# Conditional expert-weight transfers in two mixture layers of a transformer on Trainium2

## What is computed

```
# first mixture: 8 experts, top 2, each token
h = silu(x @ Wg[e].T) * (x @ Wu[e].T)         # 192 -> 768, gated
out += (h @ Wd[e].T) * w_e                    # 768 -> 192
# second mixture: 16 experts, top 2, each token
h = gelu(x @ W1[e] + b1[e])                   # 192 -> 768
y += gate_e * (h @ W2[e] + b2[e])             # 768 -> 192
```

## Time and profile before

| what | value |
|---|---|
| median of 3 runs | 3248.65 us (3239.68 to 3267.87) |
| the profiled execution | 3244.56 us |
| its span in the trace | 3242.8 us |
| mean granted TensorE clock | 0.891 |
| TensorE busy | 2612.1 us (81%) |
| VectorE, ScalarE, GpSimd busy | 43%, 28%, 13% |
| moved by DMA | 235.89 MB, of it 199.45 MB on SyncE's queue |

### The profile page before, as it was taken

The page is one execution under the profiler, slowest core; times in us unless marked ns, Lnnn a source line. Parts: engine busy times, 40 slices in busy tenths (PEclk is TensorE's granted clock), DMA queues, the critical chain, the costliest instruction groups (busy, mean ns, idle before and its releaser), DMA issues. The chain is left out here.

```text
span 3242.8 us, 52613 instructions
## 1 busy us (share of the span) xinstructions
PE 2612.1 (81%) x17466; PEld 2210.3 (68%) x17466; DVE 1405.1 (43%) x3726; ACT 913.5 (28%) x2033; POOL 405.9 (13%) x502
## 2 busy tenths in 40 slices
PE   5876999974776688883999367999678989889895
PEld 5774888873665388882888256777357777777775
DVE  2346222226776611114222743555565363553634
ACT  1220111112553133331222012444123242342421
POOL 0001223220000133330000100000011010110200
PEclk8987999996997799996999657999679989999998
DMA  3012665641001298992000000000011303113021
GB/s 87 0 27 66 183 180 178 179 134 46 0 0 40 79 281 269 284 279 72 0 0 0 2 1 14 1 0 1 10 33 32 85 0 87 29 29 87 0 80 36
DMA packets 229468, 235.89 MB, mean 73 GB/s; under 512 B 33257, under 2 KB 206111, under 8 KB 229407
## 3 DMA queue, kind: packets, MB, share of 16 engines
q1 hardware_dynamic: 208638, 199.45, 21.5%
q0 software_dynamic: 12288, 29.38, 3.0%
q10 hardware_dynamic: 8480, 6.29, 0.8%
HBM read 213.81 MB, written 21.23 MB: 72 GB/s over the span
## 5 line engine op out<-in xcount | busy, mean ns | idle before, releaser
L870 PE MATMUL f_pg<-f_vxT,f_w 128*128 128x256 f32 (+1 forms) x1536 | 274.8, 333 | 17.2 <-DMA f_b<-in_L_ffn_b 8.4
L883 PE MATMUL f_po<-f_wd,f_hid 128*128 128x192 f32 x1536 | 270.5, 330 | 12.0 <-DMA f_b<-in_L_ffn_b 7.2
L870 PEld LDWEIGHTS f_pg<-f_vxT,f_w 128*128 128x128 f32 x1536 | 240.1, 193 | 46.0 <-issue 20.1
L883 PEld LDWEIGHTS f_po<-f_wd,f_hid 128*128 128x128 f32 x1536 | 249.0, 191 | 16.8 <-ACT f_hid L921 7.7
L840 POOL DMA_INDIRECT f_answers<-f_vout,f_to_row x128 | 126.9, 991 | 461.9 <-DVE f_vout L956 247.9
L2220 PE MATMUL s_bank<-s_disp,s_w 96*128 96x256 f32 x768 | 173.1, 382 | 7.1 <-DVE s_disp L2316 7.1
L921 ACT ACTIVATE f_hid<-f_pg,f_b 128x128 f32<-128x128 f32 x384 | 112.0, 369 | 236.8 <-PE f_pg L876 121.9
L2231 PE MATMUL s_bank<-s_hid,s_w 128*96 128x256 f32 x768 | 171.0, 379 | 0.0
L2220 PEld LDWEIGHTS s_bank<-s_disp,s_w 96*128 96x128 f32 x768 | 146.6, 191 | 29.9 <-DVE s_disp L2316 8.8
L944 DVE TENSOR_TENSOR f_hid<-f_silu,f_pg 128x256 f32<-128x256 f32 x192 | 72.3, 418 | 209.1 <-ACT f_silu L917 202.9
L917 ACT ACTIVATE f_silu<-f_pg 128x256 f32<-128x256 f32 x192 | 66.9, 383 | 336.4 <-issue 249.5
(11 more groups left out here) (369 smaller groups left out, 4896.4 us busy)
## 6 DMA issues: line engine op xcount, KB each, us to landing
f_wd<-in_L_ffn_W SPq DMA_DIRECT2D x64, 576.0 KB
s_w<-in_w SPq DMA_DIRECT2D x128, 288.0 KB, 3.4
f_w<-in_L_ffn_W SPq DMA_DIRECT2D x64, 384.0 KB
f_wd<-in_L_ffn_WdT SPq DMA_DIRECT2D x32, 576.0 KB
f_w<-in_L_ffn_WgT SPq DMA_DIRECT2D x32, 384.0 KB
f_w<-in_L_ffn_WuT SPq DMA_DIRECT2D x32, 384.0 KB
f_wr<-in_L_ffn_W SPq DMA_DIRECT2D x128, 96.0 KB
f_wr<-in_L_ffn_WgT SPq DMA_DIRECT2D x64, 96.0 KB
```

The lines of the kernel that those rows point to most:

```text
L870: pe.matmul(pg[j][:, a * ROWS:(a + 1) * ROWS], lift[a][r][:, j * 128:j * 128 + 128], xT[r][:, 0, :], start=(a == 0), stop=False, skip_grou ...
L883: last = pe.matmul(po[:, c * D:c * D + D], hid[r][:, j, c * 128:c * 128 + 128], wd[r][:, j, :], start=(at == 0), stop=(at == FC - 1))
```

## The change

`route` writes a second table, `fresh`: 1 for tile n if its expert differs from that of tile n-2 (the last user of the same buffers), 0 if not, and 1 for the first two tiles.

```diff
@@ route
             nc.vector.tensor_copy(expert_of[:], tile_expert[:])
+            nc.vector.tensor_tensor(passed[:, 2:NT], tile_expert[:, 2:NT], tile_expert[:, 0:NT - 2], ALU.not_equal)
+            link(nc.vector.memset(passed[:, 0:2], 1.0))
+            nc.vector.tensor_copy(fresh[:], passed[:])
@@ experts
-            def bring_lift(n, r, e):
+            def bring_lift(n, r, e, new):
                 sp.wait_ge(lifted, (n + 1) * PER)
                 for a, src in enumerate((w_in1, w_in2) if gated else (w_in1,)):
-                    sp.dma_start(lift[a][r][:], src[ds(e, 1), 0:128]...).then_inc(loaded[r], 16)
+                    sp.dma_start(lift[a][r][:], src[ds(e, 1), 0:128]..., cond=new).then_inc(loaded[r], 16)
...
-            def bring_down(n, r, e):
+            def bring_down(n, r, e, new):
...
-            def expert(n):
-                return sp.value_load(expert_of[0:1, ds(n, 1)], min_val=0, max_val=E - 1)
-
-            bring_lift(0, 0, expert(0))
+            def of_tile(n):
+                return (sp.value_load(expert_of[0:1, ds(n, 1)], min_val=0, max_val=E - 1),
+                        sp.value_load(fresh[0:1, ds(n, 1)], min_val=0, max_val=1))
+
+            bring_lift(0, 0, *of_tile(0))
             with sp.Fori(0, NT // 2 - 1) as i:
-                e = [expert(i * 2 + r) for r in range(3)]
-                bring_lift(i * 2 + 1, 1, e[1])
-                bring_down(i * 2, 0, e[0])
+                e = [of_tile(i * 2 + r) for r in range(3)]
+                bring_lift(i * 2 + 1, 1, *e[1])
+                bring_down(i * 2, 0, *e[0])
...
```

More of the change, by code:

```diff
@@ L420, in _, with route @@
                     nc.scalar.activation(xT[u][:], split2(pT[u][0:H2, 0:2 * D]), ACT.Copy).then_inc(copied, 1)
-def route(k, name, logits, wts, place_of, expert_of, E, ROWS, probs_first):
+def route(k, name, logits, wts, place_of, expert_of, fresh, E, ROWS, probs_first):
     nc = k.nc
@@ L737, in _, with experts @@
                                            op0=ALU.add, op1=ALU.add)
-def experts(k, name, normed, answers, from_row, to_row, expert_of, E, ROWS, w_in1, w_in2, w_down, b1, b2):
+def experts(k, name, normed, answers, from_row, to_row, expert_of, fresh, E, ROWS, w_in1, w_in2, w_down, b1, b2):
     nc = k.nc
@@ L788, in _ @@
         def _(sp):
-            def bring_lift(n, r, e):
+            def bring_lift(n, r, e, new):
                 sp.wait_ge(lifted, (n + 1) * PER)
                 for a, src in enumerate((w_in1, w_in2) if gated else (w_in1,)):
-                    sp.dma_start(lift[a][r][:], src[ds(e, 1), 0:128].rearrange("o p n -> p (o n)")).then_inc(loaded[r], 16)
+                    sp.dma_start(lift[a][r][:], src[ds(e, 1), 0:128].rearrange("o p n -> p (o n)"), cond=new).then_inc(loaded[r], 16)
                     for s in range(2):
@@ L822, in _ @@
-            bring_lift(NT - 1, 1, expert(NT - 1))
-            bring_down(NT - 2, 0, expert(NT - 2))
-            bring_down(NT - 1, 1, expert(NT - 1))
+                    sp.dma_start(down_bias[r][:], b2[ds(e, 1)].broadcast_to([128, D]), cond=new).then_inc(down_loaded[r], 16)
+            def of_tile(n):
+                return (sp.value_load(expert_of[0:1, ds(n, 1)], min_val=0, max_val=E - 1),
+                        sp.value_load(fresh[0:1, ds(n, 1)], min_val=0, max_val=1))
+            bring_lift(0, 0, *of_tile(0))
@@ L826, in _ @@
+            with sp.Fori(0, NT // 2 - 1) as i:
+                e = [of_tile(i * 2 + r) for r in range(3)]
+                bring_lift(i * 2 + 1, 1, *e[1])
+                bring_down(i * 2, 0, *e[0])
+                bring_lift(i * 2 + 2, 0, *e[2])
+                bring_down(i * 2 + 1, 1, *e[1])
+            bring_lift(NT - 1, 1, *of_tile(NT - 1))
+            bring_down(NT - 2, 0, *of_tile(NT - 2))
+            bring_down(NT - 1, 1, *of_tile(NT - 1))
         @block.gpsimd
@@ L1016, in moe @@
         expert_of = k.sb(f"{name}_expert_of", [H2, tiles_of(E, ROWS)], U32, ctx=ctx)
+        fresh = k.sb(f"{name}_fresh", [H2, tiles_of(E, ROWS)], U32, ctx=ctx)
         from_row = k.sb(f"{name}_from_row", [128, slots // 128], U32, ctx=ctx)
@@ L1019, in moe @@
         norm_and_score(k, name, routerT, logits, E, keep=b2 is not None, normed=normed)
-        route(k, name, logits, wts, place_of, expert_of, E, ROWS, probs_first=b2 is not None)
+        route(k, name, logits, wts, place_of, expert_of, fresh, E, ROWS, probs_first=b2 is not None)
         tokens_of_places(k, name, place_of, from_row, to_row, slots)
-        experts(k, name, normed, answers, from_row, to_row, expert_of, E, ROWS, w_in1, w_in2, w_down, b1, b2)
+        experts(k, name, normed, answers, from_row, to_row, expert_of, fresh, E, ROWS, w_in1, w_in2, w_down, b1, b2)
         collect(k, name, answers, wts)
```

11 lines of the change are left out of this document (4 added, 7 removed).

## The result

| | before | after |
|---|---|---|
| median | 3251.34 us (22 runs) | 3259.11 us (22 runs, 3250.05 to 3266.16) |
| ratio to before | | 1.0026, 95% interval 1.0014 to 1.0038 |
| span of the profiled execution | 3242.8 us | 3257.0 us |
| moved on SyncE's queue | 199.45 MB | 130.13 MB |

The change makes the kernel slower, by a quarter of a per cent: some 8 us, where 35 were forecast. (The 3259.11 us lie just inside the forecast's 3258 to 3305 only because the median of the kernel before is now 3251.34 us, from 22 runs, and was 3248.65 from 3.

A forecast was written before the change was run, and what follows sets the result against it. SyncE's issuing was taken to bound f1: 9.95 + 2.0 + 0.96 - 0.84 = 12.07 us per turn, +38 us, plus 1.2 us of routing, on 3244.56 us: 3284 us. Its own range was 3258 to 3305, chance 0.52; overall 3238 to 3340.

The forecast's parts named there:

- What bounds f1: In f1, SyncE's instruction stream, not transfers, sets the pace: 9.8 to 10.1 us of work per two-tile turn.
- The base of the sum: SyncE's work in one f1 turn of two tiles before the change, taken as 9.95 us.
- f0: In f0, TensorE has no idle time and SyncE's wait, about 14 us per turn, hides the additions: 0 us.
- The loads: In f1, six register loads per turn instead of three, ahead of the first transfer: +2.0 us per turn.
- The condition: In f1, one more register operation per conditional transfer, 0.08 us, twelve per turn: +0.96 us.
- The skipped issue: In f1, a skipped transfer still costs SyncE 0.27 us instead of 0.41; six per turn save 0.84 us.
- Nothing is evened out: In f1, turns of 12.9 us (all fresh) to 11.2 (all skipped) stay above TensorE's 9.6, so the average counts.
- The first rival: In f1, a skip costs 0.05 us and the condition 0: -15 to +12 us, 3235 to 3257 us; chance 0.24.
- The second rival: In f1, skips cost as much as real issues, or nothing is skipped: +65 to +92 us, 3310 to 3338; chance 0.19.
- The third: In f1, transfers are the bound, so half the bytes give TensorE's 4.81 us per tile: 3207 us; chance 0.05.
- The rule that was set beside it: Skill page: initiating transfers is usually small relative to the DMA; then SyncE would not matter and bytes would bind f1.
- Routing: Three small VectorE operations on the chain in each mixture, 0.5 to 0.6 us each mixture: +1.2 us for both.

The follow-up runs named there:

- the one that fills the buffers first: Kernel before with each weight transfer moving a quarter of its columns, expert 0's weights brought once ahead of each stage: 3241.49 us, ratio 0.9963.
- the run that skips nothing: Changed kernel with the second table set to 1 throughout, so all loads and conditions stay and every transfer moves: 3308.76 us, ratio 1.0179.

## Why the prediction was right or wrong

**What bounds f1: right.** SyncE's stream is the largest part of f1's pace before the change and all of it after. The same bytes with more register loads: 37 us slower. The changed kernel with half its loads: 25 us faster. A quarter of the bytes with the same issues: SyncE's turn of 9.95 us and no wait. The base of the sum, 9.95 us, was exact. What the sum left out is that the time it is compared with is not fixed: 5.42 us per tile, 10.84 per turn, was read in the fastest of five profiles with f1 unchanged, which go up to 11.18.

**f0: right for the stage, open for the kernel.** Its expert stage is as long as before in every run but the one that fills the buffers first. SyncE's wait there covers what the change adds: 154.7 + 55.3 = 210.0 of 360 us after, 207.7 before. Yet the kernel with the change in f0 alone is slower by 12 to 20 us, and why is open.

**The loads: right.** Gap between turns 2.66 to 4.61 us, +1.95 for +2.0.

**The condition: right, a little low.** It went into the existing register operation and made it some 95 ns longer (37 to 42 before, 133 after). There are eleven of these in a turn, not twelve, because only one of the two down transfers has one:

```profile
L809 SPq DMA_DIRECT2D f_wd<-in_L_ffn_W x57: 79/388/1684, 1129.0 to 1441.0; - x57
L809 SPq FUSED_REGOPS  x28: 128/133/133, 1138.7 to 1437.7; - x28
```

That makes 1.05 us per turn for 0.96. A turn of real transfers takes 12.9 us in the run that skips nothing, as predicted (9.95 + 1.95 + 1.05 = 12.95).

**The skipped issue: this is the term that failed.** I priced it at 0.27 us by the nearest row, the register load. It takes 0.07 to 0.09 us, and 0.12 to 0.16 for the two halves of the small lift transfer. The small ones of the first tile in the turn shown above, merged there to 0.55 us, stand alone in the view of their line (ns min/median/max):

```profile
L798 SPq FUSED_REGOPS  x3: 133/133/138, 1226.3 to 1228.9; - x3
L798 SPq DMA_DIRECT2D f_wr<-in_L_ffn_W x2: 123/131/139, 1226.5 to 1226.9; - x2
```

A skipped tile thus costs 0.09 + 2 x 0.13 + 0.09 + 0.08 + 0.07 = 0.59 us in place of 2.45: 1.86 us are saved, 0.31 per transfer, where the prediction had 0.14 per transfer and 0.84 in all. Per turn, with half of the transfers skipped: 9.95 + 1.95 + 1.05 - 1.86 = 11.09 us; measured 11.19, in a window in which a little more than half were moved (30 of 57 of the first lift transfers and 31 of 57 of the down transfers, told by their duration). The forecast was 12.07. The difference, 0.9 us x 31 turns = 27 us, is as much as the forecast of +35 had too much over the measured +8. That the two agree to the us is in part luck, since the 8 us of the whole kernel are not the sum of its parts.

**Nothing is evened out: right, but closer than predicted.** The turn with all skipped takes 9.19 us (9.95 + 1.95 + 1.05 - 2 x 1.86 = 9.23 by the sum above), still SyncE's work (it doesn't wait) and not 11.2. That is no longer above the 9.6 us that the prediction gives TensorE for a turn: the margin it saw there is used up.

**The first rival (skipping nearly free)** had the truer price of a skip: 0.07 to 0.09 us, 0.13 for the small ones, for its 0.05. Its -15 to +12 us hold the measured +8. But its turns are not those of the trace: it priced the condition at 0 and had turns evened out by TensorE, where the trace has 9.19 us with all skipped for its 7.6 and, in the run that skips nothing, 12.9 for its 11.95. So its number is right partly by luck. The second rival's turn of 12.9 us appears in the run that skips nothing. The third (transfers as the pacer) is refuted by the run with more loads, by that with a quarter of the bytes, and by the changed kernel itself, which moves 102 to 165 GB/s in the two stages and gains nothing. The rule that was set beside it does not hold in this stage: the Trainium skill, page "DMA: Bandwidth & Descriptors", section "Issuing engines are not separate DMA queues", has the time to initiate a DMA as usually small relative to the DMA itself. Here the issuing instructions alone take 2 x 2.45 = 4.9 us of a turn of 10.81, and SyncE's work as a whole 9.95.

**Routing: right in kind.** The chain's end grew from 0.49 us (1076.02 to 1076.51) to 0.86 us (the cast of the expert table to the next stage's first operation), 0.37 us per mixture for 0.6.

```profile
1081.72 0.19 DVE L571 CAST f_expert_of<-f_tile_expert 96x64 uint32<-96x64 f32 x1
...
1082.58 0.27 DVE L715 TENSOR_SCALAR f_tp_hi_i<-f_place_of 96x64 int32<-96x64 int32 x1 [0.30 <-PEq L431]
```

## What to carry to other kernels

An engine that only issues has no busy time in the profile, so look at its own waits: here they were 22 of 320 us before and 1.5 after, and its instruction stream was what to shorten, while the DMA share said 0.93. Then count instructions, not bytes: merge transfers and load registers less often before you make transfers conditional. And price a branch of the sum that saves something as carefully as the ones that cost: here the costs of a turn were right to a tenth of a us, and the saving was half of its real size. Last, take a second profile of the kernel before: the scatter of one stage was 13 us here, more than the effect.

## What the runs showed that I had not expected

- A conditional transfer that is not taken costs SyncE 0.07 to 0.16 us for the instruction, and its register operation 0.13 us; one that is taken costs 0.35 as before, plus 0.1 for the register operation.
- 305 GB/s at a DMA share of 0.91 with one long row per partition, against 278 GB/s at 0.93 with six transfers per tile: the share is time that packets took, and does not say what could still be moved.
- The page's line of HBM reads is the same before and after, 213.81 MB, although 69 MB less were moved on SyncE's queue; the line of the queue shows what ran.

```profile
HBM read 213.81 MB, written 21.23 MB: 72 GB/s over the span
```
- The same code in two executions differs by 16 us of TensorE's busy time in the part behind f1 (granted clock 0.88 and 0.89), and f1's stage, with its code unchanged, takes 354.6 to 367.7 us in five profiles, with 17 to 44 us of it at the 1.2 GHz level.
